# Perceiver block with a mixture of experts on one core: down layer of experts 0 to 6 with weights standing, results turned by VectorE, last output tiles between transposes, first expert chunk by chunk

## What is computed

```python
logits = xf @ gate_w.T                       # 8 experts
top_p, top_i = jax.lax.top_k(softmax(logits), 2)
w = top_p / (sum(top_p) + 1e-09)
capacity = int(1.25 * T / 8)                 # 160 tokens per choice
rank = jnp.cumsum(one_hot(top_i), axis=0) - 1
keep = (my_rank < capacity)
for e in range(8):
    g = jax.nn.silu(xf @ gate_proj_w[e].T)   # 512 -> 1024
    u = xf @ up_proj_w[e].T
    y = g * u @ down_proj_w[e].T             # 1024 -> 512
    out = out + comb[:, e:e + 1] * y
```

## Time and profile before

| | |
|---|---|
| median of 3 runs | 1013.95 us (1012.7 to 1015.82) |
| the profiled execution's own time | 1013.0 us |
| its span, first to last instruction | 1011.2 us |
| busy: PE, PEld, DVE, ACT, POOL | 992.3 (98%), 766.5 (76%), 618.0 (61%), 397.9 (39%), 206.7 (20%) us |
| granted clock of PE over the span | 0.995 |
| chain that ended last | PE 83%, DVE 8%, DMA 6%, ACT 1% |

### The profile page before, as it was taken

How to read it: one execution, slowest core, us unless ns; L and a number is a source line. 1 busy time by engine, 2 the same in 40 slices (tenths; PEclk the granted TensorE clock), 3 DMA queues, 4 the chain that set the end, 5 groups by cost and what they waited for, 6 DMA issues and landing times.

```text
span 1011.2 us, 14027 instructions
## 1 busy us (share of the span) xinstructions
PE 992.3 (98%) x5188; PEld 766.5 (76%) x5188; DVE 618.0 (61%) x1191; ACT 397.9 (39%) x638; POOL 206.7 (20%) x188
## 2 busy tenths in 40 slices
PE   7999999999999999999999999999999999999998
PEld 4886444445554468878888888998999999999997
DVE  6268443355555566896475667577666666656666
ACT  3332211222111143355657543444454454445441
POOL 2053400002000046354322225700000000000051
PEclk9999999999999999999999999799999999999999
DMA  9809599999999932033311101884564656645443
GB/s 293 315 1 388 242 354 416 406 415 401 413 396 409 376 90 63 11 87 116 96 47 32 32 7 62 310 220 157 180 208 140 194 178 184 181 152 181 155 144 134
DMA packets 45511, 206.91 MB, mean 205 GB/s; under 512 B 5536, under 2 KB 16032, under 8 KB 41232
## 3 DMA queue, kind: packets, MB, share of 16 engines
q1 hardware_dynamic: 40256, 187.95, 51.9%
q0 software_dynamic: 5200, 18.22, 5.2%
HBM read 190.04 MB, written 16.12 MB: 204 GB/s over the span
## 4 chain that ended last, share of the span: by engine, by line
PE 83%; DVE 8%; DMA 6%; ACT 1%; issue 1%; SPq 0%; POOL 0%; ACTq 0%; DVEq 0%
PE ps L476 27%; PE ps L896 20%; PE ps L912 10%; PE ps L611 7%; PE ps L640 7%; DMA big<-in_ctxT 3%; DMA big<-in_ctx 2%; PE ps L470 2%; PE ps L588 1%; DVE stats L1282 1%; PE ps L846 1%; PE ps L937 1%; PE ps L644 1%; PE ps L621 1%; ACT w L1207 1%
## 5 line engine op out<-in xcount | busy, mean ns | idle before, releaser
L896 PE MATMUL ps<-x,w 128*128 128x320 f32 x1536 | 235.4, 309 | 2.2 <-DVE x L1865 1.1
L896 PEld LDWEIGHTS ps<-x,w 128*128 128x128 f32 x1536 | 230.0, 188 | 7.6 <-DVE w L1806 1.4
L1806 DVE TENSOR_TENSOR w<-big,w 128x1536 fp32r<-128x1536 f32 x64 | 112.4, 1758 | 80.7 <-ACT w L1207 80.2
L912 PE MATMUL ps<-w,hsplit 128*128 128x512 f32 x512 | 128.8, 393 | 0.0
L1207 ACT CAST w<-big 128x1536 fp32r<-128x1536 f32 x64 | 94.4, 1479 | 29.5 <-PE ps L912 29.5
L912 PEld LDWEIGHTS ps<-w,hsplit 128*128 128x128 f32 x512 | 93.2, 188 | 16.6
L476 PE MATMUL ps<-xcT,u 128*128 128x512 f32 x432 | 98.2, 389 | 0.0
L611 PE MATMUL ps<-big 128*64 128x512 f32 (+2 forms) x512 | 95.9, 500 | 1.0 <-DVE s_stat L1462 0.6
L476 PEld LDWEIGHTS ps<-xcT,u 128*128 128x128 f32 x432 | 81.0, 188 | 17.0 <-DVE xcT L1594 0.2
L640 PE MATMUL ps<-big 128*64 128x512 f32 x384 | 86.4, 597 | 1.7 <-DMA big<-in_ctx 1.6
L611 PEld LDWEIGHTS ps<-big 128*64 128x64 f32 x512 | 44.9, 136 | 50.2 <-issue 37.1
(11 more groups left out here) (337 smaller groups left out, 1527.6 us busy)
## 6 DMA issues: line engine op xcount, KB each, us to landing
big<-in_ctxT SPq DMA_DIRECT2D x16, 3202.0 KB, 18.9
big<-in_ctx SPq DMA_DIRECT2D x16, 3072.0 KB
big<-in_w_units SPq DMA_DIRECT2D x64, 768.0 KB, 4.3
big<-in_dense_units SPq DMA_DIRECT2D x41, 256.0 KB, 2.7
xs<-big POOLq DMA_DIRECT2D x1, 5120.0 KB, 17.5
big<-in_gate_units SPq DMA_DIRECT2D x12, 384.0 KB, 3.0
hr<-xs SPq DMA_DIRECT2D x28, 160.0 KB, 5.6
ys<-big POOLq DMA_DIRECT2D x7, 512.0 KB, 3.3
```

The lines of the kernel that those rows point to most:

```text
L896: mm = nc.tensor.matmul(ps[:, 2 * part + f % 2, 0:SLOTS], wsplit[f % RING][w][:, c:c + P], xsplit[j][x][:, d, :], start=(d == 0 and w + x ...
L912: mm = nc.tensor.matmul(ps[:, 4 + s, :], x, w, start=(f == 0 and k == 0), stop=(f == FC - 1 and k == len(terms) - 1))
L1806: V.tensor_tensor(wsplit[f % RING][1][:], wraw[f % RING], wsplit[f % RING][0][:].bitcast(F32), ALU.subtract).then_inc(w_low, 1)
```

## The change

1. **Down layer of experts 0 to 6.** The down weights stand, in four chunks of 128 output columns, and the 320 hidden values move: 4 x 3 products of 320 columns into four banks (4 to 7), output columns along the partitions. The low half of the hidden values becomes one subtraction of 320. `results_out` turns the four banks back in blocks of 32x32 (`V.transpose`) into `ye`; the host permutes the down weights so that the blocks fit, and `store` is four DMAs, one for each 32 partitions, with 512 bytes per run. `tail_out` and its buffer go. The last expert keeps the old form (`last_down`), and bank 7, which its `transpose_picks` uses, must be free first, so the first of these comes behind the first down block.
2. **Routing.** The output terms of tiles 6 and 7 are cut in pairs and set between the transposes and logits of tiles 0 to 6; on VectorE `last_apply` of tiles 5, 6 and 7 comes ahead of `choose(0)`, `choose(0)` and `pick_rows(0)`.
3. **First expert.** Its first unit starts when the first chunk is there, makes the first three chunks of both parts and then the fourth. VectorE makes the four low chunks ahead of the second weight split. The third part of expert 1's tokens is split ahead of unit 6's weights, and `pick_last_again` moves from unit 6 to unit 7.

```diff
-            transposed_tiles(0, 1)
-            for i in range(4):
-                if i < 3:
-                    transposed_tiles(i + 1, i + 2)
-                logits(0, i, 0, 3)
-            for k in range(HC):
-                output_terms(6, k)
+            for i in range(3):
+                transposed_tiles(i, i + 1)
+                if i:
+                    logits(0, i - 1, 0, 3)
+                output_terms(6, 2 * i)
+                output_terms(6, 2 * i + 1)
+            transposed_tiles(3, 4)
+            logits(0, 2, 0, 3)
+            output_terms(7, 0)
+            output_terms(7, 1)
...
+            order = [(part, d) for part in range(2) for d in range(DC)]
+            if first and f == 0:
+                order = [(part, d) for part in range(2) for d in range(DC - 1)] + [(part, DC - 1) for part in range(2)]
+            for part, d in order:
+                if first and f == 0 and part == 0:
+                    pe.wait_ge(xt_low if d else gx_low, max(d, 1))
...
+            def down(n, f, first=False):
+
+                pe.wait_ge(hid_low, n["n"] * FC + (f + 1))
+                h = [hsplit[f % 2][:, part * SLOTS:(part + 1) * SLOTS] for part in range(2)]
+                for c in range(DC):
+                    if f == 0 and not first:
+                        pe.wait_ge(y_evac, n["n"] * DC + (c - DC + 1))
+                    o = 2 * DC * P + c * P
+                    mm = three_terms(ps[:, 4 + c, 0:SLOTS], [part[:, o:o + P] for part in wsplit[f % RING]], h,
+                                     f == 0, f == FC - 1)
+                mm.then_inc(down_done, 1)
...
+                rows = ye[j].rearrange("p (s c r) -> p c s r", c=DC, r=Q)
+                for c in range(DC):
+                    V.transpose(rows[:, c, :, :], ps[:, 4 + c, 0:SLOTS].rearrange("p (s r) -> p s r", r=Q)).then_inc(y_evac, 1)
...
+                    ready = first and f - 1 == turns[-1]
+                    if ready:
+                        slots_low(n + 1, 1 - j, NS - 1)
                     if not (last and f + AHEAD >= FC):
                         split_low(n + (f + AHEAD) // FC, (f + AHEAD) % FC)
...
             split_low(0, 0)
-            split_low(0, 1)
             for d in range(DC):
                 first_expert_low(d)
+            split_low(0, 1)
             split_low(0, 2)
...
+                for q in range(P // Q):
+                    pool.dma_start(rows[:, q * P:(q + 1) * P].rearrange("(s r) w -> r s w", r=Q),
+                                   ye[j][q * Q:(q + 1) * Q, :].rearrange("p (s w) -> p s w", w=P)).then_inc(y_out[j], 16)
```

More of the change, by code:

```diff
@@ L271, in perceiver_program @@
         y_last = [rounded("y_last_high", NS * D, NS, D), rounded("y_last_low", 28800, NS, D)]
-        ye = [at(j * NS * D, NS, D) for j in range(2)]
+        ye = [at(j * NS * D, DC * SLOTS) for j in range(2)]
         SB = SLOTS // Q
@@ L891, in gate_up @@
                     pe.wait_ge(hid_done, n["n"] * FC + (f - 1))
[L892 to L899, removed]
@@ L901, in down @@
-            def down(n, f, first=False, final=False):
-                pe.wait_ge(hid_low, n["n"] * (2 * FC) + (2 * f + 2))
+                order = [(part, d) for part in range(2) for d in range(DC)]
[4 more added lines that the diff above has]
+                        pe.wait_ge(xt_low if d else gx_low, max(d, 1))
+                    c = (part * DC + d) * P
+                    mm = three_terms(ps[:, 2 * part + f % 2, 0:SLOTS], [w[:, c:c + P] for w in wsplit[f % RING]],
+                                     [x[:, d, :] for x in xsplit[j]], d == 0, d == DC - 1)
+                    if d == DC - 1:
+                        mm.then_inc(gu_done, 1)
@@ L948, in expert @@
                         gate_up(nxt, 1 - j, 0)
-                    if last:
+                    if not last:
+                        down(n, f, first)
+                        continue
+                    if f:
                         transpose_picks(f)
-                    down(n, f, first, last and f == FC - 1)
+                    last_down(f, f == FC - 1)
+                    if f == 0:
+                        transpose_picks(f)
             def nth(n, half):
                 return {"n": n, "half": half}
-            pe.wait_ge(gx_low, 1)
             gate_up(nth(0, 0), 0, 0, first=True)
@@ L1225, in picks_out, with expert @@
                                ps[:, 7, 0:NS * P].rearrange("p (s t) -> p s t", t=P)).then_inc(pick_out, 1)
-            def expert(n, j, first=False, last=False, second=False):
+            def expert(n, j, first=False, last=False):
                 for f in range(FC):
@@ L1238, in expert @@
                         picks_out(f - 1)
-                    if f == 0 and not first:
-                        tail_out(n - 1, second)
                     if not (last and f + AHEAD >= FC):
@@ L1261, in _ @@
             expert(0, 0, first=True)
-            expert(1, 1, second=True)
+            expert(1, 1)
             expert(2, 0)
@@ L1268, in _ @@
             picks_out(NT - 1)
[L1269 removed]
+            act.wait_ge(y_out[1], 64 * (NE // 2 - 1))
             for s in range(NS):
@@ L1851, in expert @@
                         pick_last_rows(2 * (f - 2))
-                    if first and f == FC - 2:
+                    if first and f == FC - 1:
                         pick_last_again()
-                    turns = (3, 4, 5) if first else (1, 3, 4)
-                    if f - 1 in turns and not last:
+                    if f - 1 in turns and not last and not ready:
                         slots_low(n + 1, 1 - j, turns.index(f - 1))
```

76 lines of the change are left out of this document (36 added, 40 removed).

## The result

The changed kernel takes 1008.68 us, the median of four executions (1007.59 to 1008.91), beside 1013.65 for the kernel before; the ratio is 0.9946, interval 0.9928 to 0.9964. The forecast was 1003.0 with a range of 999 to 1008: the direction was right, half of the gain is missing, and the time lies 0.7 us outside the range. The profiled execution of after took 1008.91 us, its span is 1007.2.

What follows compares the result with a forecast made beforehand. TensorE, busy 262.0 of 262.0 us over the experts, was taken to bound the kernel. From 1013.0 us, -4.6 - 1.24 + 0.2 - 1.2 - 3.0 gave 1003.2, told as 1003, range 999 to 1008.

Steps and rivals of the forecast that it cites:

- Term 4: Routing stage: output terms between transposes let the picks begin near 631.55 instead of 632.28, and denser; 3.0 us less.
- Term 1: Down layer of 7 experts: 12 products of 320 columns replace 8 of 512, 0.083 us less per unit; 4.6 us less.
- Terms 2 and 3: TensorE's waits ahead of the first expert (1.24 us) and for the third chunk of expert 1 (1.20 us) go.
- the charge: First expert: 0.2 us added, between 0 and 0.7, for VectorE being late with the low halves.
- B: Rival: the down blocks do not shrink, so terms 2 to 4 alone count; 1007.8 us, chance 0.10.
- C: Rival, slower: the half clock takes in the interleaved routing stretch from about 612 on; 1016.7 us, chance 0.04.
- D: Rival, slower: VectorE's turns from PSUM take 1.6 us and hold TensorE in 7 experts; 1015.5 us, chance 0.03.
- A: Rival: the clock does not fall in the routing stage, 5.9 us gained in place of 3.0; 1000.3 us, chance 0.23.

Runs made afterwards that it cites:

- early7: The changed kernel with tile 7's last four output terms straight behind its first two, ahead of the transposes of tiles 4 to 6; 1006.90 us.
- no_route: The changed kernel with the old routing order put back on TensorE and VectorE; 1007.50 us, ratio 0.9933.
- route_pool_2: The same code as route_pool, run once more on another chip beside the kernel before; 1002.06 us, ratio 0.9872.
- the third order: The changed kernel with all output terms of tiles 6 and 7 before the transposes of tiles 4 to 7, and first picks made early; 1007.94 us.
- route_pool: The changed kernel with the third order and two of GpSimd's row subtractions (tiles 5 and 6) moved; 1005.85 us, ratio 0.9922.

## Why the prediction was wrong

**Term 4 (-3.0) is the step that failed**; measured, it is between +0.2 +- 1.0 and +0.7 +- 0.7. Three statements of it were wrong. First, "the last of tile 7's output terms still ends near 626.4": the new order puts transposes of tiles 4 and 5 and logits of tile 4 ahead of it (tile 5's logits, which the text under the listing counts with them, stay behind it). The prediction left 40% of the 5.75 us of small work behind that output term; the other 60%, some 3.4 us, it charged nowhere ahead of it, setting only waits that go against waits that come. The rows of TensorE after:

```profile
616.30 0.96 PE L805 MATMUL ps<-gwT,big 128*128 128x8 f32 x8
617.11 0.71 PE L475 MATMUL ps<-u,gh 128*128 128x512 f32 x2
...
627.66 1.06 PE L805 MATMUL ps<-gwT,big 128*128 128x8 f32 x8 [0.36 <-ACT big L1002]
628.81 0.43 PE L825 MATMUL ps<-oh_rk,tri 128*128 128x64 f32 x2
...
631.21 0.60 PE L482 MATMUL ps<-ident,hr 128*128 128x128 f32 x4
...
635.83 1.88 PE L805 MATMUL ps<-gwT,big 128*128 128x8 f32 x8 [0.67 <-ACT big L1002]
637.56 0.61 PE L845 MATMUL ps<-pick,row0high 128*128 128x320 f32 x1
```

The last output term ends at 631.21, 17.2 us into the stage and not 15.0. One tile's logits cost 0.81 us (616.30 to 617.11). Some 0.3 us of the 2.2 are a wait for VectorE: the ranks that stand ahead of tile 7's last terms could follow the logits of 627.66 at about 628.5, and start at 628.81, right behind VectorE's one-hot. VectorE was held up beside GpSimd here too: tile 6's scaling took 1.50 us, and a cast 0.80, which takes 0.16 in early7. VectorE first, then GpSimd:

```profile
624.97 1.50 DVE L1309 TENSOR_SCALAR hr<-xr,mv,rstd 128x512 f32<-128x512 f32 x1 [1.63 <-POOL rstd L1920]
627.69 0.80 DVE L1727 CAST rt<-topi 128x8 f32<-128x8 uint32 x1
628.53 0.22 DVE L1728 TENSOR_TENSOR oh_rk<-eidx,rt 128x64 f32<-128x64 f32 x1
```

```profile
624.89 1.30 POOL L1998 TENSOR_TENSOR row5low<-hr,row5high 128x512 fp32r<-128x512 f32 x1
627.20 1.26 POOL L1998 TENSOR_TENSOR row6low<-hr,row6high 128x512 fp32r<-128x512 f32 x1 [1.01 <-ACT row6high L1209]
```

Second, "the picks begin near 631.55": they begin at 637.56, which is 635.08 with the late start taken off, 3.5 us later than forecast and past the 632.3 that the prediction had named as a sign of being wrong. The later output term makes 2.3 of these. The way from there to the logits of tile 7 took 4.62 us (631.21 to 635.83), as forecast (626.4 to 631.1). The logits of tile 7, which stand ahead of the picks, take 1.73 at half clock; the prediction gave them 0.45. Third, the half clock was read as a property of the order, 10.2 us long. It is one of many values that the same kernel takes, and the new order doesn't lower it. early7 shows the first statement, with what hangs on it, to be worth 2.2 +- 1.2 us of the 3.0; it is also 1.9 +- 1.3 us under no_route, which has the old order, so part of the forecast gain was there to be had. How much of the rest belongs to the logits ahead of the picks was not measured by itself.

**Term 1 (-4.6, low end 3.5)** was right in kind and a little large: 3.7 +- 0.7 measured, and 56 x 0.073 = 4.1 by the units of the trace. The down block is 1.76 us as worked out; the unit shrinks by 0.073, on the mean of the 5.28 us units, instead of 0.083. By the formula of the Trainium skill ("TensorE: Matmul & The Clock Gate", section "Back-to-back issue gap"), which that section gives for a product by itself, it would have been 5.4. The trace has 146.7 ns from product to product, and the measurement speaks against 5.4.

**Terms 2 and 3 (-1.24 + 0.2 - 1.2)** were right: 2.7 +- 0.9 measured. From the last pick to expert 1 the trace lost 2.97 us, where the two terms, the charge and eight down blocks make 2.24 + 0.66 = 2.90. About half of the charge shows too: 689.65 to 691.50 is 1.85 us instead of 1.76, and that down block starts 0.06 us behind VectorE's low half:

```profile
689.10 0.49 DVE L1858 TENSOR_TENSOR hsplit<-big,hsplit 128x320 fp32r<-128x320 f32 x1 [0.53 <-ACT hsplit L1256]
```

**Rivals.** B fell (the blocks shrank); that its 1007.8 lies nearest to the measured 1008.68 is chance, since it drops the term that was right and keeps the one that failed. C fell (613.99 to 635.84 at 1.00), D fell (0.43 us a turn, and twice that is hidden in six experts of seven). A, no fall of the clock, is real but belongs to single executions: five of route_pool_2 took 1000.84 to 1002.48 us, while the 16 executions of the changed kernel have 2 to 6 pieces each.

**The base.** The profiled execution, 1013.0 us, was one of the quicker ones: medians were 1013.65 to 1015.30, and its routing stage started at 611.51, near the early end of 611.31 to 616.11. The prediction said that the sum may be low by 1 us for that. With measured terms, 1013.65 - 3.7 - 2.7 + 0.2 to 0.7 is 1007.5 to 1008.0, against 1008.68. What the last 0.7 to 1.2 us are was not traced; single executions scatter by more.

**A faster version.** The changed kernel with the third order and GpSimd's two moves (route_pool) has medians of 1005.85 and 1002.06 us, ratios 0.9922 and 0.9872 to the kernel before, and is 8.5 to 9.4 us under it at equal half clock.

## What to carry to other kernels

Before small products are put between large ones, follow the chain that ends the stage: what has moved ahead of its first link delays all of it, and a filler is free only where TensorE would have stood still. A stretch at half clock that one profile shows is to be looked for in several executions before a term rests on it; the mean clock of each run is enough to tell them apart and to compare kernels at equal half clock. A VectorE step on the path that takes three times its usual time wants a look at GpSimd's row in the same microseconds.

## What was not expected of the hardware

- The half-clock time of one kernel differs from execution to execution, by mean clocks of 0.998 to 0.988 for the kernel before, and costs 1.44 +- 0.12 us for each 3.41 us. At equal half clock the scatter falls to a residual of 1.0 us.
- It can also fall where TensorE waits for loads (0.52 in 350 to 357 us of one profile).
- A VectorE scaling of 128x512 takes 0.55 us alone and 1.48 to 1.51 when it starts just behind a GpSimd subtraction of 128x512 (1.26 to 1.3 us).
- A turn of 128x320 out of PSUM takes 0.43 us in a row of four, less than the 0.50 worked out from turns that read SBUF.
